# Recurrence: the first two groups of columns take each gate together, and the third gate's weights are split ahead of the first sigmoids

## The reference, cut to what matters

```
i = einsum('bth,dh->btd', x, Wi); f = einsum(..., Wf); g = einsum(..., Wg)
gate = sigmoid(f)
v = silu(i) * (1.0 - gate)
o_t = gate_t * o_(t-1) + v_t              # scan over the 512 steps
o = o * rsqrt(mean(o*o) + eps) * gnorm_w * g * sigmoid(g)
x = layernorm(x + einsum('btd,hd->bth', o, Wo))
```

## Time and profile before

| | |
|---|---|
| median of 3 runs | 2553.0 us (2551.19 to 2557.34) |
| the profiled execution, its own time | 2558.96 us |
| its span, first to last instruction | 2557.2 us |
| mean granted TensorE clock | 0.980 |
| PE busy | 2399.1 us, 94% of the span |
| recurrence, until the first transfer of the next stage | about the first 225 us |

### The profile page before, as it was taken

One profiled execution on the slowest core, in us unless ns is written; L12 is line 12 of the kernel. 1 busy time (PEld: TensorE's weight loads), 2 busy tenths in 40 slices (PEclk: granted clock), 3 DMA queues, 4 the chain that ended last, 5 costly groups with the idle time before them and its releaser, 6 DMA issues. The chain is left out here.

```text
span 2557.2 us, 39125 instructions
## 1 busy us (share of the span) xinstructions
PE 2399.1 (94%) x15376; PEld 1547.3 (61%) x15376; DVE 1353.7 (53%) x2114; ACT 1348.8 (53%) x1708; POOL 919.3 (36%) x608
## 2 busy tenths in 40 slices
PE   7997899989999999999997999998899999999997
PEld 5885644444444444444333555555578899999885
DVE  5566634434344434434413556555475577776785
ACT  4221467666767777767895434433332266665221
POOL 1223744655355544655202333332034012121320
PEclk8998999999999999999999999999899999999999
DMA  5002675576547653775653300001045267775430
GB/s 181 17 1 72 192 224 126 126 197 170 141 116 209 168 153 93 180 203 143 173 124 104 111 1 1 18 18 53 34 140 170 90 228 233 243 244 186 152 113 37
DMA packets 206983, 331.46 MB, mean 130 GB/s; under 512 B 71312, under 2 KB 125840, under 8 KB 206608
## 3 DMA queue, kind: packets, MB, share of 16 engines
q1 hardware_dynamic: 188304, 252.80, 34.9%
q0 software_dynamic: 16336, 72.23, 8.6%
q10 hardware_dynamic: 2160, 3.93, 0.6%
HBM read 241.53 MB, written 99.42 MB: 133 GB/s over the span
## 5 line engine op out<-in xcount | busy, mean ns | idle before, releaser
L938 ACT ACTIVATE A_c_prob<-c_psum 128x1024 f32<-128x1024 f32 x832 | 787.1, 1029 | 285.9 <-PE c_psum L1188 273.0
L864 POOL TENSOR_TENSOR c_rr<-c_ms,c_half 128x32 f32<-128x32 f32 (+1 forms) x72 | 372.6, 5177 | 426.4 <-DVE c_ms L955 424.8
L1197 PE MATMUL c_psum<-A_c_prob,c_vq 128*17 128x512 f32 x3328 | 417.0, 601 | 8.3 <-DVE c_oT L1092 8.1
L134 PE MATMUL c_psum<-R_c_w,S_c_c 128*128 128x512 f32 x1248 | 313.9, 401 | 0.7 <-DVE S_c_c L966 0.5
L1188 PE MATMUL c_psum<-c_qq,c_kq 64*128 64x512 f32 x1664 | 288.3, 438 | 26.6 <-DMA c_vq<-vd 14.5
L134 PEld LDWEIGHTS c_psum<-R_c_w,S_c_c 128*128 128x128 f32 x1248 | 227.9, 189 | 121.9 <-issue 40.7
L1188 PEld LDWEIGHTS c_psum<-c_qq,c_kq 64*128 64x128 f32 x1664 | 136.9, 186 | 175.6 <-ACT A_c_prob L938 92.6
L995 DVE COPY Q_c_unit<-c_psum 128x256 f32<-128x256 f32 x89 | 37.8, 425 | 333.6 <-PE c_psum L134 333.6
L2363 PE MATMUL m_psum<-A_m_dn_hi,A_m_a 128*128 128x512 f32 (+1 forms) x628 | 204.4, 394 | 2.4 <-DVE A_m_a L2160 2.4
L134 PE MATMUL m_psum<-R_m_t,m_up_hi 128*128 128x256 f32 (+1 forms) x1104 | 200.0, 283 | 0.0
L1616 DVE TENSOR_REDUCE s_topx<-s_psum 128x4 f32<-128x2048 f32 (+1 forms) x64 | 95.5, 1493 | 172.2 <-PE s_psum L1719 167.5
(11 more groups left out here) (298 smaller groups left out, 4282.1 us busy)
## 6 DMA issues: line engine op xcount, KB each, us to landing
c_kq<-kd SPq DMA_DIRECT2D x248, 208.0 KB, 6.1
kd<-S_c_t SPq DMA_DIRECT2D x96, 256.0 KB
Q_c_raw<-in_ctxT SPq DMA_DIRECT2D x89, 256.0 KB
qd<-A_c_q SPq DMA_DIRECT2D x64, 256.0 KB
c_qq<-qd SPq DMA_DIRECT2D x64, 256.0 KB, 3.1
vd<-A_c_vt SPq DMA_DIRECT2D x104, 136.0 KB, 4.1
c_vq<-vd SPq DMA_DIRECT2D x31, 442.0 KB, 9.1
R_m_hs<-slots SPq DMA_DIRECT2D x23, 512.0 KB
```

The costliest lines, as they stand in the source:

```text
L134: mm = pe.matmul(out, a(c), b(c), start=first and i == 0, stop=last and i == len(terms) - 1)
L864: pool.tensor_tensor(rr[:, unit % RB, 0:n], ms[:, unit % RB, 0:n], half[:, 0:n], ALU.pow).then_inc(s_r, 1)
L938: act.activation(prob[:, t % PB, 2 * (u % 2):2 * (u % 2) + 2, :], score_banks[u % 3], ACT.Exp, scale=XD ** -0.5).then_inc(s_ex, 1)
L1197: mm = pe.matmul(o_bank[32 * j:32 * j + VW, :], vq[:, q % 2, kt, j, :], prob[:, t % PB, j, :], start=kt == 0, stop=kt == CT - 1)
```

## The change

PE takes gate(0, 0), gate(1, 0), gate(0, 1), gate(1, 1), gate(0, 2), gate(1, 2), and goes on as before from n = 2. `place` gives each gate's position in that order, by which ACT waits. On ACT the split of Wg stands directly behind that of Wf, ahead of the sigmoids of group 0; on DVE its low part stands ahead of everything of group 0. The banks and the loads are as before.

```
+        place = lambda n, g: 2 * g + n if n < 2 else 3 * n + g
...
-                    act.wait_ge(s_gate, n * 3 + g + 1)
+                    act.wait_ge(s_gate, place(n, g) + 1)
...
                 if n == 0:
                     split_w(1)
+                    split_w(2)
                 sigmoids(n, (0, 1, 2))
-                if n == 0:
-                    split_w(2)
                 sigmoids(n, (3,))
...
                 dve.tensor_tensor_scan(o[:, q, :], sig[:, q, 1, :], v[:], 0.0, ALU.mult, ALU.add).then_inc(s_o, 1)
-                if n == 0:
-                    split_w(2)
...
             split_w(1)
+            split_w(2)
             for n in range(B * KC):
...
-                if n == 0 and g:
+                if n < 2 and g:
                     pe.wait_ge(s_wlo, g)
...
-            for n in range(B * KC):
+            for g in range(3):
+                for n in range(2):
+                    gate(n, g)
+            for n in range(2, B * KC):
                 for g in range(3):
                     gate(n, g)
```

## The result

The changed kernel's median is 2543.57 us over 7 runs (2538.59 to 2547.89). The kernel before, run 7 times for this comparison, has 2558.22 us (2551.19 to 2561.77). The ratio is 0.9948, with a 95% interval of 0.9934 to 0.9962: faster by 0.52%, between 0.38% and 0.66%. The prediction was 12.8 us or 0.50%. The runs of one kernel differ by 9 to 11 us, so the time alone says little about the single steps. Those have to be read from the traces.

A forecast was written before the change was run, and what follows sets the result against it. PE paces the recurrence and never regains its start losses. Second pause 5.4, filled part of the first 2.8 and faster matmuls some 4.6 give 12.8 us: 2553.0 - 12.8 = 2540.2 us, range 2534 to 2548.

The forecast's parts named there:

- The size: At the start of gate(2, 0): 30.2 us against 43.04, a gain of 12.8 us that reaches the whole time.
- The 4.6 us for the slow matmuls of gates (0, 1) and (0, 2): These 24 matmuls took 5.2 and 4.96 us and would take 2.8 a gate at full clock, some 4.6 us gained.
- The level of 2540.2: The whole kernel's forecast time: the median of 2553.0 us less the gain of 12.8 us.
- The first pause: PE before gate(0, 1): gate(1, 0) fills 2.8 of the 4.34 us, about 1.55 us remain.
- The second pause and the cycle: PE before gate(0, 2): 5.4 us vanish, as Wg's split waited for PE and PE for Wg's split.
- rival 4: At the start, Wf's low part alone bounds; only gate(1, 0)'s 2.8 us are won, time 2550 us; chance 0.02.
- The clock over the remaining pause: PE before gate(0, 1): the clock stays full over the 1.55 us; if it fell, the gain would be 9.7 to 10.5.
- Wg's landing and the slack: Before gate(0, 2): Wg lands at 18.6 us, its split ends at 22.8, with 1.8 us to spare.
- The chain behind: After gate(0, 2), from `sg` to `v` of group 2: done at 42.6 us, wanted by gate(3, 2) at 44.2, 1.6 spare.
- The ride to the end: From gate(2, 0) to the next stage, behind a barrier of all engines: the 12.8 us arrive whole, first load at 212.4.
- Rival 3: In the next stage, more clock falls at about 1.6 us each make the kernel slower, over 2561 us; chance 0.02.

The follow-up runs named there:

- run 7: Not a run's label: in "run 7 times" it counts measurements of the unchanged kernel before, median 2558.22 us, against the changed kernel's 2543.57, ratio 0.9948.
- the experiment: The next batch's x loaded ahead of Wg, against the changed kernel: 2542.01 us against 2554.37 for the kernel before the change, ratio 0.9954.

## Why the prediction was right

**The size.** 12.8 us were predicted. At the start of gate(2, 0) the traces give 12.0 between the two first profiles and 12.3 between the means of two and four executions. At the next stage's first load it is 12.1 and 12.8; the last half microsecond, which makes the number exact, comes from the stretch of the last projection, where the change does nothing, and is luck. The 4.6 us for the slow matmuls of gates (0, 1) and (0, 2) were those of one execution: in the second execution of before the clock rose sooner in both gates (at 22.9 and 33.0), and the same sum gives 3.3. The level of 2540.2 was 3.4 us under the first median, because the kernel before had itself risen from 2553.0 to 2558.2 with more runs; the difference was the right thing to take. In time the gain came out at 14.7, 11.7 and 12.3 us between the medians of the three comparisons (ratios 0.9948, 0.9956 and 0.9950).

**The first pause.** I expected 1.55 us to remain. It was none, 0.90, 0.88 and 1.68 in the four executions. Wf's landing differs (15.32, 14.75, 14.77 and 14.23), and so does the moment when the clock rises: at 18.6, 15.4, 15.4 and some 12.2 us, by the change of pace from 0.427 to 0.233. A late rise makes gate(1, 0) slower and the pause shorter by the same amount, because gate(0, 1) waits for the low part of Wf in any case. Gate(0, 1) started 0.06 us behind that low part in three executions and 0.24 behind it in the first, so even the latest rise cost only 0.2 us. I had put this at about 1 us of spread. The gain follows the landing of Wf instead: with Wf landing 0.5 us earlier than in the second execution, the fourth had gate(2, 0) at 29.83 against 30.35.

**The second pause and the cycle.** The size was right, the cause in part. The order alone left 2.62 us of the pause, the early split alone removed it, and the early copy without the early subtraction left 3.07. I had written, against rival 4, that the new order breaks the cycle; it is the early split that does, VectorE's part of it above all.

**The clock over the remaining pause.** Right, and with more pauses than the earlier trace rows gave: it held over 0.88, 0.90, 1.19 (in the kernel with the next x ahead), 1.54, 1.63 and 1.68 us, and fell over 2.62 and 3.07. The warning of the Trainium skill ("TensorE: Matmul & The Clock Gate", section "A second HAM failure mode: psum-queue depth-cycling") about short idles between groups of matmuls did not come true for the pauses up to 1.68 us at this place. One step of my reasoning was unsound, and in the first execution its outcome failed too: I took the clock at 14.4 as full from the column that reads 1.00 over 9.00 to 14.60. In the trace of before, matmuls start 0.43 us apart until 13.6 in that same window. The profile after reads 1.00 over the stretch from 14.40 to 17.20 too, where matmuls start 0.427 apart:

```profile
14.40:17.20 2.80, 2.80 (x7) 2.22 (x8) 0.00 (x0) 1.88 (x1) 0.00 (x0) 1.00 0.57 128
```

Seven matmuls in 2.8 us are little more than half of the 12 that fit at full clock. So ahead of the first change that it shows, the column can't be read here. What kept the sum right is that gate(0, 1) waits for the low part of Wf at either pace.

**Wg's landing and the slack.** I had 18.6 for the landing; it was 19.58, 18.72, 18.97 and 18.26 in the four executions. The slack was 25.4 - 23.8 = 1.6 us in the first, and 1.5 to 1.7 by the experiment, against 1.8.

**The chain behind.** Expected 1.6 us to spare at gate(3, 2), measured 45.0 - 43.4 = 1.6. No pause of PE came of it in any run.

**The ride to the end.** Right: 12.04 us at gate(2, 0) were 12.14 at the next stage's first load. That the span fell by 15.8 is within the spread behind it. Rival 3, more falls of the clock in what follows, does not show: behind the first load the changed kernel took 2320.6 to 2328.3 us, the kernel before 2325.0 and 2332.0.

## What to carry to other kernels

When an engine waits for a preparation that itself stands behind results of that engine, both a different order of the main work and an earlier place for the preparation shorten the wait. Here each shortened a different pause: the order filled the first and left 2.62 us of the second, the early split removed the second and left the first. Each alone is therefore worth a run of its own; how their gains add up was not settled. A preparation may be put ahead of a queue's other work, even with a wait of 2.35 us in it, if the time by which those others are wanted is worked out for each of them. A gain at the start of this program of stages behind barriers arrived whole at the next stage, but it was hardly larger than the spread of runs. The start of the next stage in the trace spread over 2.1 us in four executions of the changed kernel, and the start of gate(2, 0), close behind the change, over 1.2 us; both say more than a single time does. By time, seven runs of each kernel gave 0.38% to 0.66%.

## What the runs showed of the hardware

The moment at which TensorE's clock rises varied by 6 us between executions of one kernel (matmul starts go from 0.427 to 0.233 us apart at 12.2, 15.4, 15.4 and 18.6 us). The profile's column for the granted clock reads 1.00 in stretches with matmuls 0.427 us apart, in all of these executions (14.40 to 17.20 in the first profile after) and until 25 us in that of the early split alone. In the pauses between gates, up to 1.68 us kept the full clock; 2.62 us lost it (0.52 over the next 6.4 us), and so did 3.07 us, for less (0.66 over 4.6 us). The stretch behind the recurrence, the same code throughout, spread over 12.8 us (2320.6 to 2333.4) in twelve executions.
